# A state-space layer on one core: the causal mask of the decay moved to TensorE, dt applied as a per-partition scalar

## What is computed

```
a = dt * A;  cs = cumsum(a)                       # over the chunk's 128 tokens
Ldec = where(tri, exp(cs[q] - cs[k]), 0)          # keys k not later than query q
att  = (C[q] . B[k]) * Ldec
Yd   = att @ (X * dt[k])                          # within the chunk
dec_end = exp(cs[last] - cs[k])
states  = sum over k of dec_end[k] * B[k] * X[k] * dt[k]
state   = exp(cs[last]) * state + states          # carried to the next chunk
Y = Yd + (C . previous state) * exp(cs[q]) + D * X
```

## Time and profile before

| | us |
|---|---|
| median of three executions | 495.55 (494.87 to 496.28) |
| the profiled execution | 494.94 |
| its span | 493.2 |
| TensorE busy (TensorE's mean granted clock 0.994) | 473.5 (96%) |
| VectorE busy | 316.8 (64%) |
| ScalarE busy | 236.8 (48%) |
| GpSimd busy | 215.1 (44%) |

### The profile page before, as it was taken

One profiled execution on the slowest core, in us unless ns is written; L12 is line 12 of the kernel. 1 busy time (PEld: TensorE's weight loads), 2 busy tenths in 40 slices (PEclk: granted clock), 3 DMA queues, 4 the chain that ended last, 5 costly groups with the idle time before them and its releaser, 6 DMA issues.

```text
span 493.2 us, 6223 instructions
## 1 busy us (share of the span) xinstructions
PE 473.5 (96%) x2104; PEld 377.1 (76%) x2104; DVE 316.8 (64%) x518; ACT 236.8 (48%) x444; POOL 215.1 (44%) x242
## 2 busy tenths in 40 slices
PE   8998999988999989999999899999999999999995
PEld 7886677765767768888788778888888888888884
DVE  3793587746688856677998889865957523411223
ACT  5887667766556666455343245234805430033300
POOL 5835476526773596767877000010004442133321
PEclk9998999999999999999999999999999999999998
DMA  7531022003212415342332166410300000200001
GB/s 247 200 110 49 38 86 65 21 23 102 75 59 86 167 45 193 130 171 86 130 105 83 69 214 213 170 45 7 122 21 1 0 0 1 85 2 0 2 15 70
DMA packets 14431, 40.80 MB, mean 83 GB/s; under 512 B 2368, under 2 KB 2368, under 8 KB 14400
## 3 DMA queue, kind: packets, MB, share of 16 engines
q1 hardware_dynamic: 14400, 40.41, 24.1%
HBM read 38.30 MB, written 2.10 MB: 82 GB/s over the span
## 4 chain that ended last, share of the span: by engine, by line
PE 80%; DVE 11%; issue 4%; ACT 3%; POOL 2%; POOLq 0%; DVEq 0%
PE psA L1621 8%; PE psA L1622 8%; PE psA L1410 6%; PE psA L1412 6%; PE psB L1631 4%; PE psB L1630 4%; PE psA L1416 3%; PE psA L1418 3%; PE psA L1600 3%; PE psA L1599 3%; PE psA L1596 3%; DVE xbc L1168 3%; PE psB L1596 2%; PE psB L1600 2%; PE psB L1599 2%
## 5 line engine op out<-in xcount | busy, mean ns | idle before, releaser
L1621 PE MATMUL psA<-xT_h,q_gu 128*128 128x512 f32 x176 | 70.1, 398 | 0.0
L1622 PE MATMUL psA<-xT_l,q_gu 128*128 128x512 f32 x176 | 69.1, 393 | 0.0
L669 POOL TENSOR_SCALAR var<-mv 128x1 f32<-128x1 f32 x16 | 4.9, 305 | 128.7 <-DVE mv L1060 128.6
L1031 ACT ACTIVATE gate_t<-psA 128x512 f32<-128x512 f32 x22 | 13.2, 598 | 75.1 <-PE psA L1622 75.1
L816 POOL TENSOR_TENSOR int_l<-prod_t,int_h 128x512 fp32r<-128x512 f32 x22 | 28.7, 1306 | 45.7 <-ACT int_h L1036 45.7
L1362 DVE TENSOR_TENSOR prod_t<-gate_t,psA 128x512 f32<-128x512 f32 x22 | 15.1, 689 | 51.7 <-PE psA L1622 48.6
L727 POOL TENSOR_TENSOR beta<-wsum,beta 128x512 fp32r<-128x512 f32 x28 | 36.1, 1312 | 24.8 <-ACT beta L892 24.8
L1621 PEld LDWEIGHTS psA<-xT_h,q_gu 128*128 128x128 f32 x176 | 33.1, 188 | 8.2
L1622 PEld LDWEIGHTS psA<-xT_l,q_gu 128*128 128x128 f32 x176 | 33.1, 188 | 7.4
L1631 PE MATMUL psB<-q_dn,int_l 128*128 128x512 f32 x88 | 34.3, 389 | 0.0
L1630 PE MATMUL psB<-q_dn,int_h 128*128 128x512 f32 x88 | 34.2, 389 | 0.0
(11 more groups left out here) (251 smaller groups left out, 1358.8 us busy)
## 6 DMA issues: line engine op xcount, KB each, us to landing
raw<-in_f_gu_t SPq DMA_DIRECT2D x22, 512.0 KB, 3.3
raw<-in_w_gu_t SPq DMA_DIRECT2D x14, 512.0 KB, 3.8
raw<-in_f_dn_t SPq DMA_DIRECT2D x10, 512.0 KB, 3.6
raw<-in_w_gu_t SPq DMA_DIRECT2D x14, 256.0 KB, 2.9
raw<-in_w_dn_t SPq DMA_DIRECT2D x7, 512.0 KB, 3.3
raw<-in_w_in_t SPq DMA_DIRECT2D x5, 512.0 KB, 4.4
x<-in_hidden SPq DMA_DIRECT2D x8, 256.0 KB, 4.9
out<-x SPq DMA_DIRECT2D x8, 256.0 KB, 2.0
```

The lines of the kernel that those rows point to most:

```text
L1621: nc.tensor.matmul(ps, w, seq(xT_h, k, b), start=k == 0, stop=False)
L1622: done = nc.tensor.matmul(ps, w, seq(xT_l, k, b), start=False, stop=k == KD - 1)
```

## The change

A third accumulating pass joins `seg` in PSUM. `masking` is -256 times the identity, so masking^T strict puts -256 wherever the key is later than the query, for all four heads at once (a head-broadcast of `strict` as the moving operand); exp then gives zero there. `seg` itself is zero at these places, since `until` holds no token that is both after the key and not after the query. The triangle is so no longer needed in VectorE's product. dt comes in as a scalar per partition: in the product of `decay` with C B, now one scalar_tensor_tensor for each head, and in a product of four columns that writes `wend`. GpSimd's `dt_until` and its two semaphores go; GpSimd makes `masking` at the start. On TensorE the bank for `seg` is opened, and the mask pass issued, ahead of the wait for `until`.

```diff
+            nc.gpsimd.memset(masking[:].bitcast(F32), 0.0)
             link(nc.gpsimd.memset(strict[:].bitcast(F32), 1.0))
+            nc.gpsimd.affine_select(out=masking[:], in_=masking[:], compare_op=ALU.not_equal, fill=-256.0, base=0,
+                                    pattern=[[-1, P]], channel_multiplier=1)
...
-                if t >= 1:
-                    pool.wait_ge(dt_taken, t)
-                nc.gpsimd.tensor_tensor(heads(dt_until[:]), tri[:].unsqueeze(1).to_broadcast([P, H, P]),
-                                        dtT[:, b, H * c:H * c + H].unsqueeze(2).to_broadcast([P, H, P]), ALU.mult)\
-                    .then_inc(dt_until_ready, 1)
...
                     v.wait_ge(*freed_b(("seg", b, c)))
-                    v.wait_ge(dt_until_ready, t + 1)
-                    nc.vector.tensor_tensor(decay[:], decay[:], dt_until[:], ALU.mult).then_inc(dt_taken, 1)
-                    v.wait_ge(dt_taken, t + 1)
+                    v.wait_ge(dt_ready, b + 1)
                     if c < NC - 1:
...
-                        nc.vector.tensor_copy(wend[:, t % 2, :], heads(decay[:])[:, :, P - 1]).then_inc(wend_ready, 1)
+                        nc.vector.tensor_tensor(wend[:, t % 2, :], heads(decay[:])[:, :, P - 1],
+                                                dtT[:, b, H * c:H * c + H], ALU.mult).then_inc(wend_ready, 1)
                         v.wait_ge(wend_ready, i + 1)
                     job = ("cb", b, c)
                     v.wait_ge(*done_b(job))
-                    nc.vector.tensor_tensor(decay[:], bank_b(job), decay[:], ALU.mult).then_inc(freed_b(job)[0], 1)
+                    for h in range(H):
+                        last = nc.vector.scalar_tensor_tensor(
+                            out=decay[:, chunk(h)], in0=decay[:, chunk(h)], scalar=dtT[:, b, H * c + h:H * c + h + 1],
+                            in1=bank_b(job)[:, chunk(h)], op0=ALU.mult, op1=ALU.mult)
+                    last.then_inc(freed_b(job)[0], 1)
...
+                    ps = open_b(("seg", b, c))
+                    nc.tensor.matmul(heads(ps), masking[:], strict[:].unsqueeze(1).to_broadcast([P, H, P]),
+                                     start=True, stop=False)
                     pe.wait_ge(until_ready, 2 * (NC * b + c + 1))
-                    ps = open_b(("seg", b, c))
-                    nc.tensor.matmul(ps, strict[:], until_h[:], start=True, stop=False)
+                    nc.tensor.matmul(ps, strict[:], until_h[:], start=False, stop=False)
                     nc.tensor.matmul(ps, strict[:], until_l[:], start=False, stop=True).then_inc(b_done, 1)
```

More of the change, by code:

```diff
@@ L362, in layer_kernel @@
         (win_h, win_l, xbc0, sz0, xbc1, sz1, wout_h, wout_l, decay, ecs, xnbn, xs, state, yt, yt_h, yt_l, diag_d,
-         dt_until, tri, strict, until_h, until_l, xT_f, t_f, ln2_sb, nrm2) = overlay(
+         masking, tri, strict, until_h, until_l, xT_f, t_f, ln2_sb, nrm2) = overlay(
             ("win_h", 0, [P, NIN, RAW], F32R), ("win_l", 20480, [P, NIN, RAW], F32R),
@@ L370, in layer_kernel @@
             ("yt_h", 111616, [P, H * P], F32R), ("yt_l", 113664, [P, H * P], F32R),
-            ("diag_d", 115712, [P, H * P], F32), ("dt_until", 117760, [P, H * P], F32), ("tri", 119808, [P, P], BF16),
+            ("diag_d", 115712, [P, H * P], F32), ("masking", 117760, [P, P], F32R), ("tri", 119808, [P, P], BF16),
             ("strict", 120064, [P, P], F32R), ("until_h", 120576, [P, H * P], F32R),
@@ L413, in layer_kernel @@
         until_ready = sem("until_ready")
-        dt_until_ready = sem("dt_until_ready")
-        dt_taken = sem("dt_taken")
         att_ready = sem("att_ready")
```

## The result

The changed kernel took 491.67 us in the median of four executions (491.24 to 492.14), the kernel before 495.21 beside it: a ratio of 0.9925, with an interval of 0.9911 to 0.9939. Forecast were 495.2 us and a range of 493.3 to 497.6. So in this comparison the changed kernel is faster by 0.75%, where I had forecast no difference to speak of. Over the whole study eleven executions of the changed kernel have a median of 492.69 us and 58 of the kernel before 495.46, 2.8 us (0.56%) apart; the forecast sum was -0.39.

The account below looks back on a forecast made before the run. TensorE, busy 473.5 of 493.2 us, was taken as the bound. Start +0.39, mask passes +1.57 and stalls -0.75, -0.6, -0.3, -0.7 summed to -0.39: 495.2 us from 495.55, range 493.3 to 497.6.

Parts of the forecast that it names:

- The start, +0.39: Kernel start: GpSimd's extra memset and affine_select delay TensorE's warm-up by 0.39 us, with nothing found to absorb it.
- The mask pass, 0.23 us: TensorE's added matmul per chunk: 0.23 us where fed, 0.42 in (sequence 0, chunk 0), nothing at (1,0) and (1,1); sum +1.57.
- (0,3)'s norm, -0.75: Sequence 0, chunk 3: L1241 without GpSimd's collision takes about 0.75 instead of 1.52 us, shortening TensorE's 1.2 us wait by 0.75.
- (1,0), -0.6: Sequence 1, chunk 0: earlier `xs` and `decay` let the diagonal's add end sooner, releasing L1534 0.6 us earlier.
- (1,2), -0.3: Sequence 1, chunk 2: the 0.3 us wait for the C B bank goes, as the last product ends 0.30 earlier.
- (1,3), -0.7: Sequence 1, chunk 3: VectorE gains 0.8 us ahead of state update L1206, so TensorE's 0.7 us wait goes.
- (0,1): Sequence 0, chunk 1: TensorE is fed there, so the mask pass costs +0.23 us; no stall gives anything back.
- those 3.7 us are all that a faster decay path can win in the scans: TensorE's listed waits in the two state-space scans total 3.7 us, taken as the limit of any gain there.
- part 4: GpSimd: eight `dt_until` passes of 1.04 to 1.49 us go; VectorE operations colliding with GpSimd passes can take twice their time.
- B: Rival, slower: GpSimd, free earlier, collides with VectorE operations TensorE needs in sequence 1; +2.0, 497.5 us; chance 0.18.
- C: Rival, faster: the half-rate clock stretch behind the 1.9 us wait goes; -2.7, 492.9 us; chance 0.12.
- D: Rival, slower: the mask pass takes 0.86 instead of 0.23 us, six times on the path; +3.8, 499.0 us; chance 0.04.

Follow-up runs that it names:

- experiment 6: Changed kernel timed again: ratio 0.9953; with the mask tile made behind the other constants: 0.9933; that plus 14 identity transposes before the first chunk's wait: 0.9936.
- before_wend: Kernel before, with `wend` made first from undivided decay and dt, the two 512-column products behind it: 494.89 us, ratio 0.999.
- after_one: Changed kernel with one 512-column product of decay and C B in place of the four, leaving dt out: 492.71 us in one execution.
- before_no_pass: Kernel before without GpSimd's `dt_until` pass; VectorE's product reads `diag_d` instead, so the decay is wrong: 493.50 us, ratio 0.9952.
- before_again: Kernel before, unedited, profiled once more on one chip with the changed kernel: 496.19 us in one execution.
- before_fill: Kernel before, with 14 identity transposes on TensorE ahead of its wait for `xbc` in sequence 0's first chunk: 494.93 us, ratio 0.9992.

## Why the prediction was wrong

By its own steps:

- **The start, +0.39: not shown.** The warm-up begins 0.38 us later, as forecast. But I passed the whole shift on to the end. The warm-up's end also hangs on when the clock rises, which the prediction didn't know of; at an unmoved rise the shift costs about 0.2 us by the estimate in experiment 6. Under a spread of 1.6 us no timing settles it. The sums below keep the 0.39.
- **The mask pass, 0.23 us: right in size,** 0.19 to 0.24 measured. The sum was +1.57, and 0.98 came. (0,0) was charged at half rate, +0.42, for 0.21: one execution's chance was taken for the kernel's. In (0,3) I charged 0.23 ahead of the wait for the norm, of which I kept 0.45 in the same sum: a pass that ends ahead of a wait that remains only fills it (0.31 us left with the pass, 0.56 without). (1,3) took 0.10 for 0.23. That nothing is paid at (1,0) and (1,1) was right.
- **(0,3)'s norm, -0.75: right.** From cb (0,3) to the norm's transposes 16.60 us became 15.82, -0.78, and three kernels show this to be GpSimd's pass (0.77 to 0.78). With the mask I had forecast -0.52.
- **(1,0), -0.6: right,** -0.58, partly by luck: I gave `xs` its 1.04 us without asking what it would run beside, and beside an SBUF product, as in before_wend, it takes 1.55.
- **(1,2), -0.3: right.** The stretch lost 0.09; with the mask's 0.24 that is -0.33. The wait left the list but isn't gone: after_one wins another 0.22 there.
- **(1,3), -0.7: too small a term.** The stretches lost 1.08 with the mask in them, -0.78 and -0.30, where I had -0.7 + 0.23. The list gives a wait of 0.7 us, but the pass with `until_h` started 1.76 us behind cb (143.70 to 141.94) and starts 1.14 behind it now, with the mask between them (140.47 to 139.33): 0.62 us less. The whole stretch lost 0.78, and 0.10 more had gone to the mask, so about 0.9 us hung on that chain, of which before_no_pass gives the GpSimd pass 0.50. A wait in the list is counted from the modelled end of the matmul before it. These are TensorE's rows there, in the kernel before and in the changed one:

```profile
141.94 1.02 PE L1503 MATMUL psB<-xbc 128*128 128x512 f32 x2
143.70 0.47 PE L1508 MATMUL psB<-until_h,strict 128*128 128x512 f32 x1 [0.73 <-DVE state L1206]
```

```profile
139.33 1.02 PE L1502 MATMUL psB<-xbc 128*128 128x512 f32 x2
140.13 0.49 PE L1506 MATMUL psB<-strict,masking 128*128 128x512 f32 x1
140.47 0.39 PE L1509 MATMUL psB<-until_h,strict 128*128 128x512 f32 x1
```

And the bank that follows the norm's transposes was late by 0.3 more in the kernel before, which I hadn't charged.
- **(0,1): the step that failed.** I wrote that "those 3.7 us are all that a faster decay path can win in the scans", and that TensorE is fed in (0,1): +0.23. It lost 0.98. That miss of 1.2 us is half of the 2.3 us between the forecast sum and -2.7. The list was taken from an execution in which (0,0) had run at half rate. This made TensorE 1.5 us late, and so it found the bank ready for which it waits 0.9 us in before_again (and before_fill, at full rate too, has the long stretch again, 14.22). A stall that another delay covers isn't absent from the kernel. Of the 0.98, before_no_pass gives the GpSimd pass 0.74; put back it costs 0.49 to 0.51. The mask takes 0.19 back. So 0.43 to 0.67 us remain for VectorE's own shorter path, of which `wend` alone, in before_wend, gives 0.20; how the rest divides is not settled, since the effects overlap in one wait.

So of the 2.3 us between -0.39 and -2.7, 1.2 come from (0,1), 0.6 from (1,3), 0.26 from (0,3) and 0.2 from (0,0); the others cancel. The first timing (-3.5) lay 0.8 us lower still. That fits the spread of the start and of the half rates, since the changed kernel gave 491.67, 493.53 and 493.67 in three groups, but the executions that were only timed have no trace that would show it.

The rivals. B had a GpSimd freed earlier collide more; the sign was the other way, the pass that left took its collisions with it, and no new one reached the path. (At 111.02 VectorE's L1101 takes 1.32 us beside `until_h`, where it takes 0.68 at its shortest, as B had it, but the stretches from there on don't get longer by it.) C named the half rate, which did vanish in the first profile, but it comes and goes whatever the kernel, and filling the wait leaves the distance between the kernels as it was. D is out by the mask's 0.19 to 0.24. My own theory of GpSimd (part 4) had the mechanism, and I applied it to L1241 and L1097 alone. L746 was 1.04 to 1.49 us long eight times; what to do was to look beside each of the eight for the VectorE operations that were longer than their median. The trace of the kernel before has one beside the second pass, among the small steps ahead of (0,1):

```profile
53.96 1.09 DVE L1144 TENSOR_SCALAR dtw<-dtw 128x16 f32<-128x16 f32 x1 [0.91 <-ACT dtw L928]
```

## What to carry to other kernels

A pass taken off a GpSimd that is half idle can be worth more than its place on any list of waits says: look beside each of its occurrences for VectorE operations that take several times their shortest, however small they are, and follow what is queued behind them. Read a kernel's stalls from two executions at least, and compare milestones start to start; an execution in which the clock made TensorE late hides the stalls behind that place. Where a producer is moved earlier, check what its consumer then runs beside: `wend` 0.7 us sooner was worth 0.2 with a product of two SBUF tensors behind it, and 0.6 together with a single product that reads PSUM.

## What the runs showed of the hardware

- VectorE steps of 128x16 take 0.17 us alone. One with its tensors in SBUF that begins beside a GpSimd pass of 128x512 lasts until that pass ends: 0.83 to 1.09 us in the longest cases, scalar and single-input forms among them (L1149, a tensor_scalar, 0.96). One that reads PSUM isn't held: in before_again L1138 took 0.17 at 51.85, beside the pass L798 that then held L1141 for 1.04. A loss of 0.8 us doesn't need a large operation.
- It goes in both directions: GpSimd's `xs` takes 1.55 us for 1.04 when a VectorE product of two SBUF tensors starts 0.04 us ahead of it, and 1.04 beside four of 128 columns that read PSUM.
- The warm-up's length is partly chance: 4.86 to 6.46 us for the same 30 transposes, which start 0.21 us apart until the trace's first record of the clock and 0.11 after it. The first C B moves with it, from 45.8 to 47.5 us in the changed kernel, whose times lie between 491.2 and 494.1.
- After a wait of 1.6 to 2.1 us ahead of (0,0) TensorE ran the next 3.7 us at a granted clock of 1.00 in 12 of 14 profiles and at 0.54 or 0.55 in two, the kernel before and a variant of the changed one (+1.5 us). After one of 1.8 us behind the scans 7 of 17 had a stretch at 0.50 (+0.5 us).
